# Relation pass of a graph network: eight per-relation comparisons with a lane number written as one comparison with a table

## The chip, the cores and the metric

One NeuronCore of a Trainium2 chip runs the whole program. The metric is the device time of one launch in microseconds; the time of a kernel is the median of its runs.

## What is computed

Four graph layers one after another on 3125 nodes of 64 features and 100000 edges, with a residual and a layer norm behind each: attention (three rounds), an edge MLP with a mean over incoming edges, a relational layer with eight weight matrices, and a graph convolution with signed edge weights. The change touches the third:

```
x_src = x[src]
out = zeros
for r in range(8):
    msg = where(edge_type == r, x_src @ weight[r], 0)
    out = out + segment_sum(msg, dst, num_segments=3125)
out = relu(out + x @ self_loop_w.T)
x = layernorm(x + out)
```

## The kernel before

Edges are sorted once into slots: 13 triples of destination bins by 25 source tiles give 325 chunks of three tiles with 128 slots each (`NCHUNK`, `SLOTS`, `P`). Every later layer runs `edge_pass` over these chunks. For each chunk it must fetch a row per edge, and then add the rows up by destination, which is a matmul with a one-hot matrix of destinations.

In the relation pass (`kind == "relations"`, tag `rp`) a row is x[src] @ weight[type]. Of every five chunks, two are fetched: GpSimd gathers 3 x 128 rows from the table `rel_rows` in DRAM (L1306, 130 chunks, eight slots ahead). The other three (positions 0, 2 and 4 of five, 195 chunks in all) are looked up by TensorE. Their steps are:

- `spell` on TensorE (L1560): three matmuls spread the chunk's 384 keys over all 128 partitions of a PSUM bank. A key is 128 times the relation plus the source node's number within the tile.
- `take_key` on ScalarE (L1487): copies them to `key_rows`, fp16, two buffers.
- `hot_source` on VectorE (L1344): for each relation r compares `key_rows` with the lane number 128 r + p of partition p and writes the one-hot `hot_src`, bf16, eight times 384 columns, two buffers (`HOT_SLOTS`).
- `look_up` on TensorE (L1577): 24 matmuls, 3 tiles by 8 relations, of `hot_src` with `rel_pieces` (each table value in three bf16 parts).
- `take_rows` on ScalarE (L1495, L1497): copies the result to `msg`.
- `hot_target` on VectorE (L1353): the one-hot of destinations, for every chunk. `add_up` on TensorE (L1605, L1607 for looked-up chunks, L1611 for fetched ones) adds up in PSUM.

The order on each engine is written out. In iteration c, TensorE does `spell(c + 6)`, `look_up(c + 3)`, `add_up(c)`; VectorE does `hot_source(c + 3)`, `hot_target(c)`; ScalarE does `take_key(c + 4)`, `take_rows(c + 1)`. Semaphores tie them: `hot_source` of the n-th looked-up chunk waits for `key_taken` of n and for `looked_up` of n - 2; `look_up` waits for `hot_made` of n; `take_key` waits for `spelled` of n and `hot_made` of n - 2; GpSimd waits for `added` of the fetched chunk eight back. Before the loop VectorE waits for the first leftover record, computes `left_number`, and makes the first two one-hots.

Of the kernel before, what the change touches and what calls it, by code (L numbers as in the profile page):

```python
# [5 lines left out]
FP16 = mybir.dt.float16  # L6
# [4 lines left out]
ALU = mybir.AluOpType  # L11
# [3 lines left out]
P = 128  # L15
# [4 lines left out]
RELS = 8  # L20
# [12 lines left out]
SLOTS = 3  # L33
# [129 lines left out]
class Program:  # L163
# [57 lines left out]
    def sb(self, name, shape, dtype=FP32):  # L221
        return self.ctx.enter_context(self.nc.sbuf_tensor(name, shape, dtype))
# [911 lines left out]
def over_columns(a, count):  # L1134

    return a.unsqueeze(2).broadcast_to([a.shape[0], a.shape[1], count])
# [13 lines left out]
def edge_pass(k, tag, kind, pieces, table, width, cols):  # L1150
# [12 lines left out]
    HOT_SLOTS = 2 if relations else 8  # L1163
# [8 lines left out]
    with ExitStack() as ctx, semaphores(nc, tag) as sem:  # L1172
        sb = lambda name, shape, dt=FP32: ctx.enter_context(nc.sbuf_tensor(f"{tag}_{name}", shape, dt))
        described, spelled, hot_made, looked_up = sem("described"), sem("spelled"), sem("hot_made"), sem("looked_up")
# [15 lines left out]
        if relations:  # L1190
            rows = sb("rows", [P, ROW_SLOTS, SLOTS, width])
            key_rows = sb("key_rows", [P, 2, SLOTS * P], FP16)
            hot_src = sb("hot_src", [P, 2, RELS, SLOTS * P], BF16)
            hot_dst16 = sb("hot_dst16", [P, DST_SLOTS, SLOTS, BIN_ROWS], BF16)
            msg = sb("msg", [P, MSG_SLOTS, SLOTS, 3 * D], BF16)
        else:
            hot_src = sb("hot_src", [P, HOT_SLOTS, SLOTS * P], BF16)
            msg = sb("msg", [P, MSG_SLOTS, SLOTS, cols])
# [37 lines left out]
        with nc.Block() as block:  # L1236
# [82 lines left out]
            def _(dve):  # L1319
                v, chain = nc.vector, Chain(dve, step)  # L1320
# [17 lines left out]
                def hot_source(c):  # L1338
                    n = LOOKUP_NO[c]
                    dve.wait_ge(key_taken, n + 1)  # L1340
                    if n >= HOT_SLOTS:
                        dve.wait_ge(looked_up, n - HOT_SLOTS + 1)
                    for rel in range(RELS):
                        last = v.tensor_scalar(hot_src[:, n % HOT_SLOTS, rel, :], key_rows[:, n % 2, :],  # L1344
                                               k.lane[:, rel:rel + 1], None, ALU.is_equal)
                    last.then_inc(hot_made, 1)

                def hot_target(c):
                    if c >= DST_SLOTS:
# [39 lines left out]
                def left_number():  # L1389
                    if relations:  # L1390
                        v.scalar_tensor_tensor(left_no[:, :], left_rec[:, H + 3:H + 4], float(RELS),
                                               left_rec[:, H + 5:H + 6], ALU.mult, ALU.add).then_inc(left_idx, 1)
                    else:
                        v.tensor_copy(left_no[:, :], left_rec[:, H + 3:H + 4]).then_inc(left_idx, 1)
# [39 lines left out]
                dve.wait_ge(left_in, 16)  # L1434
                left_number()
                if relations:
                    for c in range(3):
                        if looks_up(c):
                            hot_source(c)
                if kind == "near":  # L1440
                    weigh(0)
                for c in range(NCHUNK):
                    if edges and c % FILL == 0 and c // FILL + READ_AHEAD < NCHUNK // FILL:
                        describe(c // FILL + READ_AHEAD)
                    if relations and c + 3 < NCHUNK and looks_up(c + 3):
                        hot_source(c + 3)
                    hot_target(c)
                    if kind == "near" and c + 1 < NCHUNK:
                        weigh(c + 1)
                    if not relations:  # L1450
                        message(c)

                left_count = dve.value_load(k.left_tiles[0:1, 0:1], min_val=1, max_val=EPAD // P)
                with dve.Fori(0, left_count) as i:
# [4 lines left out]
                    for b in range(LEFT_BANKS):  # L1459
# [6 lines left out]
                        first, n = 4 * b, min(4, NT - 4 * b)  # L1466
# [3 lines left out]
                        last = v.tensor_tensor(to, to, bank[:, 0:n, 0:main], ALU.add)  # L1470
                    if edges:
                        last = v.tensor_tensor(k.acc[:, :, H:FIELD], k.acc[:, :, H:FIELD],
                                               k.psum[:, 7, 0:NT * 3].rearrange("p (t c) -> p t c", c=3), ALU.add)
# [679 lines left out]
def program(nc, dram, out):  # L2153
    with ExitStack() as ctx:
# [16 lines left out]
        with nc.sbuf_tensor("edge_pieces", [P, NT, 3, FIELD], BF16) as pieces:  # L2171
            edge_table(k, pieces)
            edge_pass(k, "ep", "edges", pieces, k.edge_rows, H, FIELD)
        edge_mean(k)
        node_mlp(k)
        with nc.sbuf_tensor("rel_pieces", [P, looked_up, RELS, 3 * D], BF16) as pieces:
            with nc.sbuf_tensor("rel_rest", [P, LOOKED_UP, RELS * D], FP32) as k.rel_rest:
                relation_table(k, pieces)
            edge_pass(k, "rp", "relations", pieces, k.rel_rows, D, D)
        with nc.sbuf_tensor("near_pieces", [P, NT, 3, D + 2], BF16) as pieces:  # L2180
            with nc.sbuf_tensor("near", [P, NT, D + 2], FP32) as k.near:
                near_table(k, pieces)
            edge_pass(k, "sp", "near", pieces, k.near_rows, D + 2, H)
# [59 lines left out]
```

## Time and profile before

| | us |
|---|---|
| median of 3 runs | 4437.56 (4431.42 to 4444.34) |
| profiled execution | 4402.9 |
| its span | 4401.2 |
| VectorE busy in the span | 3220.0 |
| TensorE matmuls busy in the span | 3083.2 |
| GpSimd busy in the span | 1408.1 |

The relation pass is the stretch from about 2834 to 3495 us of the span. In the rows further down, times are in microseconds from the span's start, PE is TensorE's matmuls, DVE VectorE, ACT ScalarE and POOL GpSimd. A bracket or the part behind a bar tells how long the engine was idle before the instruction and what is thought to have ended that; "issue" means that the view found no releaser. Some semaphore records are missing from a trace, so a real wait can appear as "issue", or under the name of a DMA of another pass.

### The profile page before, as it was taken

The page shows a single profiled execution, that of the slowest core. Times are in us where ns is not written, and L with a number is a line of the kernel's source. Part 1 is how long each engine was busy: PE and PEld are TensorE (multiplying, and loading weights), DVE is VectorE, ACT ScalarE, POOL GpSimd, SP SyncE. Part 2 cuts the span into 40 slices and gives each one's busy share as a digit, 9 for nine tenths or more (in the row PEclk, how much of TensorE's full clock was granted, in tenths as well). Part 3 has the DMA queues.
Part 4 walks back from the last instruction along what each step waited for, and adds up shares of the span by engine and source line. Part 5 has one row for each costly group of instructions (what it writes and reads, how often), then busy time and mean ns, then how long its engine had stood idle before and what let it go on. Part 6 is the DMA issues. An engine that isn't in the chain of part 4 may idle for free. (4 is left out here: it accounts for less than half of the span.)

```text
span 4401.2 us, 85012 instructions
## 1 busy us (share of the span) xinstructions
PE 3083.2 (70%) x29186; PEld 2395.9 (54%) x29186; DVE 3220.0 (73%) x7812; ACT 1438.3 (33%) x2737; POOL 1408.1 (32%) x1203
## 2 busy tenths in 40 slices
PE   0077777787228338338499996588888769968996
PEld 0044554454102102112299995278888759958996
DVE  7766666666389799789577774277777679977887
ACT  0034444444115125125299992233333200000000
POOL 0055555555254464464000000166666300000000
PEclk9988888888569669669699996599999979989998
DMA  8844555545458448458366660111111023313332
GB/s 319 339 129 133 164 149 157 160 132 154 141 168 260 143 136 265 125 162 262 108 216 220 217 207 15 66 23 25 24 24 24 17 66 109 107 41 100 91 90 56
DMA packets 414245, 587.75 MB, mean 134 GB/s; under 512 B 76564, under 2 KB 302443, under 8 KB 413445
## 3 DMA queue, kind: packets, MB, share of 16 engines
q1 hardware_dynamic: 366293, 448.13, 33.9%
q0 software_dynamic: 37888, 67.18, 5.4%
q10 hardware_dynamic: 9648, 67.01, 3.7%
q8 instruction: 247, 4.05, 0.4%
q14 instruction: 169, 1.38, 0.1%
HBM read 340.53 MB, written 235.00 MB: 131 GB/s over the span
## 5 line engine op out<-in xcount | busy, mean ns | idle before, releaser
L848 POOL DMA_INDIRECT slots<-bc_rec,idx x496 | 485.6, 979 | 390.4 <-ACT bc_rec L808 275.3
L1108 PE MATMUL psum<-a_probs,z 128*65 128x512 f32 (+1 forms) x1050 | 448.2, 561 | 141.9 <-DVE a_probs L1041 141.8
L1344 DVE TENSOR_SCALAR rp_hot_src<-rp_key_rows,lane 128x384 bf16<-128x384 f16 x1560 | 382.2, 315 | 175.6 <-issue 80.8
L1577 PE MATMUL psum<-rel_pieces,rp_hot_src 128*128 128x192 bf16 x4680 | 438.7, 248 | 72.6 <-issue 55.6
L1306 POOL DMA_INDIRECT rp_rows<-rel_rows,slot_rel x390 | 410.8, 1053 | 224.0 <-issue 86.5
L1076 ACT ACTIVATE a_tops<-a_tops,a_s_low 128x1024 f32<-128x1024 f32 (+2 forms) x300 | 284.0, 947 | 568.6 <-DVE a_tops L1032 568.3
L484 POOL DMA_INDIRECT slots<-h,idx x192 | 328.9, 1713 | 353.5 <-DMA h<-recs 305.1
L1577 PEld LDWEIGHTS psum<-rel_pieces,rp_hot_src 128*128 128x128 bf16 x4680 | 386.0, 99 | 96.8 <-issue 74.7
L1108 PEld LDWEIGHTS psum<-a_probs,z 128*65 128x65 f32 x1050 | 122.2, 138 | 468.4 <-DVE a_probs L1041 296.6
L704 DVE TENSOR_SCALAR bc_first_t<-bc_ramp,bc_key_t 128x128 f16<-128x128 f16 x500 | 135.3, 271 | 306.0 <-PE psum L730 175.4
L1032 DVE SCALAR_TENSOR_TENSOR a_tops<-table,a_s_rest,big 128x1024 f32<-128x1024 f32 (+2 forms) x300 | 306.9, 1023 | 32.0 <-DMA big<-shift_rows 31.8
L730 PE MATMUL psum<-bc_first_s,bc_first_t 128*128 128x512 f16 x1000 | 217.3, 378 | 111.5 <-DVE bc_first_s L705 62.2
L1041 DVE SCALAR_TENSOR_TENSOR a_probs<-a_tops,a_counts 128x1024 f32<-128x1024 f32 (+2 forms) x300 | 288.2, 962 | 0.0
L1611 PE MATMUL psum<-ep_msg,ep_hot_dst 128*84 128x131 f32 x1950 | 278.3, 278 | 7.7 <-ACT ep_msg L1503 5.8
L1611 PE MATMUL psum<-sp_msg,sp_hot_dst 128*84 128x128 f32 x1950 | 280.0, 280 | 0.0
L1611 PE MATMUL psum<-sq_msg,sq_hot_dst 128*84 128x128 f32 x1950 | 272.4, 276 | 0.0
L1584 PE MATMUL psum<-far_pieces,sq_hot_src 128*128 128x128 bf16 x2925 | 218.1, 220 | 29.5 <-DMA sq_hot_src<-hot_rows 29.5
L705 DVE TENSOR_SCALAR bc_first_s<-bc_ramp,bc_key_s,bc_base_s 128x625 f16<-128x625 f16 x500 | 238.7, 477 | 0.0
L1101 PE MATMUL psum<-ident,a_shifts 128*50 128x128 f32 x3 | 1.2, 410 | 330.5 <-DVE a_shifts L1023 330.5
L1584 PE MATMUL psum<-edge_pieces,ep_hot_src 128*128 128x131 bf16 x2925 | 228.6, 223 | 2.2 <-ACT ep_hot_src L1520 2.2
L1611 PEld LDWEIGHTS psum<-ep_msg,ep_hot_dst 128*84 128x84 f32 x1950 | 221.7, 154 | 10.2 <-DVE ep_hot_dst L1353 9.3
L1374 DVE TENSOR_TENSOR ep_sums<-psum,ep_rec 128x393 f32<-128x393 f32 x325 | 183.7, 565 | 58.6 <-PE psum L1584 58.0
(459 smaller groups left out, 6697.1 us busy)
## 6 DMA issues: line engine op xcount, KB each, us to landing
a_counts<-edge_counts SPq DMA_DIRECT2D x150, 512.0 KB
slots<-big ACTq DMA_DIRECT2D x65, 1005.0 KB
ep_rec<-slots SPq DMA_DIRECT2D x65, 1005.0 KB, 7.5
edge_counts<-bc_counts SPq DMA_DIRECT2D x12, 3125.0 KB
hot_rows<-ep_hot_src SPq DMA_DIRECT2D x325, 96.0 KB, 4.6
sp_hot_src<-hot_rows SPq DMA_DIRECT2D x325, 96.0 KB, 2.1
sq_hot_src<-hot_rows SPq DMA_DIRECT2D x325, 96.0 KB, 2.0
a_counts<-edge_counts SPq DMA_DIRECT2D x75, 282.5 KB
```

Of the source, the lines that this page charges most:

```text
L484: pool.indirect_dma_start(k.slots, bass.IndirectOffsetOnAxis(k.idx[:, at:at + 1], 0), self.rows[y][:, t, :], None).then_inc(self.scattered ...
L705: last = v.tensor_scalar(to_s[:, u, :], ramp[:, :], column(key_s, t), column(base_s, j), ALU.subtract, ALU.is_equal)
L848: pool.indirect_dma_start(k.slots, bass.IndirectOffsetOnAxis(k.idx[:, first + t:first + t + 1], 0), rec[:, j, t, :], None).then_inc(scatte ...
L1032: v.scalar_tensor_tensor(tops[:, cols], shift_1[:, cols], s_rest[:, s:s + 1], shift_2[:, cols], ALU.add, ALU.max).then_inc(topped, 1)
L1041: v.scalar_tensor_tensor(probs[:, cols], tops[:, cols], 1.0, counts[:, cols], ALU.min, ALU.mult)\
L1076: nc.scalar.activation(tops[:, cols], tops[:, cols], ACT.Exp, bias=s_low[:, s:s + 1])\
L1108: last = nc.tensor.matmul(sums[:, a:b], k.z[:, s, 0:D + 1], probs[:, a:b], start=s == 0, stop=True, skip_group_check=True)
L1306: pool.indirect_dma_start(rows[:, n % ROW_SLOTS, s, 0:width], None, table, bass.IndirectOffsetOnAxis(k.slot_rel[:, at:at + 1], 0))\
L1344: last = v.tensor_scalar(hot_src[:, n % HOT_SLOTS, rel, :], key_rows[:, n % 2, :], k.lane[:, rel:rel + 1], None, ALU.is_equal)
L1577: last = nc.tensor.matmul(to, hot_src[:, n % HOT_SLOTS, r, s * P:(s + 1) * P], pieces[:, row, r, :], start=s != 1 and r == 0, stop=True, s ...
L1584: last = nc.tensor.matmul(got[:, s, :], hot_src[:, n % HOT_SLOTS, s * P:(s + 1) * P], pieces[:, row, piece, :], start=s == 0 and piece == ...
L1611: last = nc.tensor.matmul(to[:, 0:D] if relations else to, hot_dst[:, y, s, :], got, start=first, stop=True, skip_group_check=True)
```

## The change

Three edits. A table `lanes` of 8 x 384 fp16 values per partition is added to SBUF. Before the first one-hot, one tensor_copy fills it by repeating each of the eight lane numbers 384 times, and VectorE waits for its end. In `hot_source` the eight tensor_scalars are replaced by one tensor_tensor over 3072 elements per partition: one source is `key_rows`, read eight times over by a broadcast, the other is `lanes`; the result goes to the same `hot_src`. `hot_made` is raised by that one instruction.

```diff
@@ -1191,6 +1191,7 @@
             rows = sb("rows", [P, ROW_SLOTS, SLOTS, width])
             key_rows = sb("key_rows", [P, 2, SLOTS * P], FP16)
             hot_src = sb("hot_src", [P, 2, RELS, SLOTS * P], BF16)
+            lanes = sb("lanes", [P, RELS, SLOTS * P], FP16)
             hot_dst16 = sb("hot_dst16", [P, DST_SLOTS, SLOTS, BIN_ROWS], BF16)
             msg = sb("msg", [P, MSG_SLOTS, SLOTS, 3 * D], BF16)
         else:
@@ -1340,10 +1341,9 @@
                     dve.wait_ge(key_taken, n + 1)
                     if n >= HOT_SLOTS:
                         dve.wait_ge(looked_up, n - HOT_SLOTS + 1)
-                    for rel in range(RELS):
-                        last = v.tensor_scalar(hot_src[:, n % HOT_SLOTS, rel, :], key_rows[:, n % 2, :],
-                                               k.lane[:, rel:rel + 1], None, ALU.is_equal)
-                    last.then_inc(hot_made, 1)
+                    shape = [P, RELS, SLOTS * P]
+                    v.tensor_tensor(hot_src[:, n % HOT_SLOTS, :, :], key_rows[:, n % 2, :].unsqueeze(1).broadcast_to(shape),
+                                    lanes[:, :, :], ALU.is_equal).then_inc(hot_made, 1)
 
                 def hot_target(c):
                     if c >= DST_SLOTS:
@@ -1434,6 +1434,7 @@
                 dve.wait_ge(left_in, 16)
                 left_number()
                 if relations:
+                    chain.link(v.tensor_copy(lanes[:, :, :], over_columns(k.lane[:, :], SLOTS * P)))
                     for c in range(3):
                         if looks_up(c):
                             hot_source(c)
```

`over_columns(a, count)` repeats each column of a `count` times by a broadcast (step 0 innermost).

## Rows read from the trace of the kernel before

**Rows 1.** The page, busy tenths of PE and DVE in 40 slices.
```profile
PE   0077777787228338338499996588888769968996
...
DVE  7766666666389799789577774277777679977887
```

**Rows 2.** Busy time by stretch: window, its length, engines with instruction counts, clock, DMA.
```profile
2854.00:2869.00 15.00, 2.59 (x10) 1.63 (x11) 2.58 (x10) 0.75 (x3) 9.04 (x10) 0.50 0.12 23
2900.00:3465.00 565.00, 496.28 (x6377) 470.86 (x6376) 426.85 (x1661) 201.55 (x527) 364.56 (x345) 1.00 0.11 25
3471.00:3490.00 19.00, 19.00 (x261) 19.00 (x261) 17.42 (x70) 8.14 (x23) 0.00 (x0) 1.00 0.01 3
```

**Rows 3.** Groups by line and form, 2834 to 3495: busy us, mean ns, idle before.
```profile
L1577 PE MATMUL psum<-rel_pieces,rp_hot_src 128*128 128x192 bf16 x4680 | 438.7, 248 | 72.6 <-issue 55.6 <-DVE rp_hot_src L1344 15.7
L1306 POOL DMA_INDIRECT rp_rows<-rel_rows,slot_rel x390 | 410.8, 1053 | 224.0 <-issue 86.5 <-PE psum L1611 85.4 <-DMA rel_rows<-big 52.2
...
L1344 DVE TENSOR_SCALAR rp_hot_src<-rp_key_rows,lane 128x384 bf16<-128x384 f16 x1560 | 382.2, 315 | 175.6 <-issue 80.8 <-DMA marks_now<-edge_marks 57.3 <-ACT rp_key_rows L1487 35.7
```

**Rows 4.** Timeline of DVE, one period: start, length, instruction, count, idle before.
```profile
3158.97 1.95 DVE L1344 TENSOR_SCALAR rp_hot_src<-rp_key_rows,lane 128x384 bf16<-128x384 f16 x8 [2.38 <-issue]
3160.84 0.41 DVE L1353 TENSOR_TENSOR rp_hot_dst<-bin_lane,slot_dst 128x252 f32<-128x252 f32 x1
3161.17 1.91 DVE L1344 TENSOR_SCALAR rp_hot_src<-rp_key_rows,lane 128x384 bf16<-128x384 f16 x8
...
3168.70 1.95 DVE L1344 TENSOR_SCALAR rp_hot_src<-rp_key_rows,lane 128x384 bf16<-128x384 f16 x8 [2.46 <-issue]
```

**Rows 5.** Timeline of PE in the same period.
```profile
3160.97 2.15 PE L1577 MATMUL psum<-rel_pieces,rp_hot_src 128*128 128x192 bf16 x24 [1.21 <-issue]
...
3166.29 0.33 PE L1560 MATMUL psum<-ident,slot_key 128*128 128x128 f16 x3
...
3170.70 0.51 PE L1577 MATMUL psum<-rel_pieces,rp_hot_src 128*128 128x192 bf16 x4 [1.34 <-issue]
```

**Rows 6.** Timeline of PE: first and last of the 47 lookups behind their comparisons.
```profile
2876.91 0.83 PE L1577 MATMUL psum<-rel_pieces,rp_hot_src 128*128 128x192 bf16 x8 [0.21 <-issue]
...
3468.55 0.67 PE L1577 MATMUL psum<-rel_pieces,rp_hot_src 128*128 128x192 bf16 x6 [1.20 <-issue]
```

**Rows 7.** Timeline of ACT in the period, the key copies.
```profile
3158.44 0.87 ACT L1487 ACTIVATE rp_key_rows<-psum 128x384 f16<-128x384 f32 x2 [1.50 <-PE psum L1560]
...
3168.17 0.87 ACT L1487 ACTIVATE rp_key_rows<-psum 128x384 f16<-128x384 f32 x2 [0.74 <-DMA marks_now<-edge_marks]
```

**Rows 8.** Single lines of DVE: count, shortest/median/longest in ns, first and last start.
```profile
L1344 DVE TENSOR_SCALAR rp_hot_src<-rp_key_rows,lane x1560: 299/309/526, 2834.0 to 3492.3; 128x384 bf16<-128x384 f16 x195
...
L1353 DVE TENSOR_TENSOR rp_hot_dst<-bin_lane,slot_dst x325: 400/407/417, 2837.7 to 3493.5; 128x252 bf16<-128x252 f32 x99, 128x252 f32<-128x252 f32 x64
...
L1407 DVE TENSOR_SCALAR big<-all_rows,rp_left_rec x1: 1047/1047/1047, 3493.9 to 3493.9; 128x3200 bf16<-128x3200 int16 x1
...
L1940 DVE TENSOR_TENSOR edge_pieces<-big,edge_pieces x1: 3493/3493/3493, 2169.6 to 2169.6; 128x3200 bf16<-128x3200 f32 x1
```

**Rows 9.** Timeline of PE, two lookups a period apart after the last gather.
```profile
3471.06 2.14 PE L1577 MATMUL psum<-rel_pieces,rp_hot_src 128*128 128x192 bf16 x24
...
3479.22 2.14 PE L1577 MATMUL psum<-rel_pieces,rp_hot_src 128*128 128x192 bf16 x24
```

**Rows 10.** Two casts of DVE from 32 to 16 bits.
```profile
L2047 DVE CAST rel_pieces<-rel_rest x5: 959/959/960, 2758.8 to 2828.2; 128x1536 bf16<-128x1536 f32 x5
...
L1937 DVE CAST edge_pieces<-table x1: 3465/3465/3465, 2159.0 to 2159.0; 128x3200 bf16<-128x3200 f32 x1
```

**Rows 11.** Timeline of DVE, the first comparisons of the pass.
```profile
2834.04 3.78 DVE L1344 TENSOR_SCALAR rp_hot_src<-rp_key_rows,lane 128x384 bf16<-128x384 f16 x16
```

**Rows 12.** Timeline of POOL in the period, two gathers.
```profile
3161.35 1.85 POOL L1306 DMA_INDIRECT rp_rows<-rel_rows,slot_rel  x1 [0.30 <-issue]
3163.85 0.94 POOL L1306 DMA_INDIRECT rp_rows<-rel_rows,slot_rel  x1 [0.65 <-PE psum L1611]
```

## The prediction

> **What bounds the kernel now.** I read the page's slices first. The edit touches one pass only, the relation pass, which fills about 660 us of the 4401 us span; in its slices TensorE (PE) and VectorE (DVE) are both high and neither is full [rows 1]. The chain that ended last covers the final layer alone, so it can't price this pass. Next the busy time by stretch: between 2900 and 3465 us PE is busy 496.28 of 565 us and DVE 426.85 us, at a granted clock of 1.00 [rows 2]. So PE stands idle 68.7 us there, and no faster DVE can give back more than what of that idleness is a wait for DVE. The groups by form give the sizes: the 1560 comparisons of L1344 fill 382.2 us, that is 1.96 us for each of the 195 groups of eight; PE is idle 72.6 us before its lookup matmuls; the gathers of GpSimd (POOL) take 1053 ns on average [rows 3].
>
> Then the timeline of one period (five chunks, three looked up). DVE compares in groups of eight: 3158.97 for 1.95 us, the next at 3161.17, and the pattern comes again at 3168.70 [rows 4]. A period is thus 9.73 us. PE starts a lookup at 3160.97, 0.05 us after the first of those groups ends (3158.97 + 1.95 = 3160.92), after 1.21 us of idleness; at 3170.70 the same after 1.34 us (3168.70 + 1.95 = 3170.65) [rows 5]. The view names "issue" there; by the times it is the hot_made wait of `look_up`. The two other groups of a period end well before their lookups. I counted this through the pass: 47 of the 195 lookups, at most one in a period of 65, start within 0.1 us of the end of their comparisons after an idle stretch, 46.0 us in all; the first and the last are shown [rows 6]. Two more at the start of a period add 3.1 us.
>
> Why is that group late? It starts right behind the key copy of ScalarE (ACT): copies at 3158.44 and 3168.17, comparisons 0.53 us later. And the copy itself waited: 1.50 us for L1560 before 3158.44 [rows 7], although PE had issued the last spelling of a period at, for instance, 3166.29 for 0.33 us [rows 5] and the copy came at 3168.17 [rows 7]. PE's signals come late here. They do so only while POOL gathers: after the last gather, from 3471 to 3490, PE is busy 19.00 of 19 us with POOL at 0.00 [rows 2], and a period is 3479.22 - 3471.06 = 8.16 us [rows 9].
> So the loop is: lookup, spelling, late signal, key copy, comparisons, lookup. The comparisons count once in it, in 47 of 65 periods.
>
> **The change part by part.** *Eight tensor_scalars out.* One takes 309 ns at the median for 384 elements, and L1407 takes 1047 ns for 3200 [rows 8]: (1047 - 309) / 2816 = 0.26 ns an element, so each pays some 0.10 us for data and 0.13 us of its 0.23 us spacing for being an instruction (1.87 us from 3158.97 to 3160.84, by eight) [rows 4]. What goes is 1.96 us a group, with the disturbed ones in it.
>
> *One tensor_tensor of 3072 elements in.* The trace holds no tensor_tensor whose operands are all of 16 bits. With a 32-bit operand, 252 elements take 407 ns and 3200 take 3493 ns [rows 8]: 1.047 ns an element and 0.144 us fixed. At that rate 3072 elements take 3.36 us. At two elements in that time they take 1.61 + 0.14 = 1.75 us. These are the two ends: 1.75 and 3.36 us. Nothing in the trace suggests a form below 1.75 (that would be the rate of tensor_scalar). I take 1.75: the tensor_scalars with 16-bit operands run four elements in the time in which the mixed forms run one, so packing of 16-bit values is at work in this program, both sources have step 1 innermost, and the width change alone should give the factor of two. That choice is the weak point and is the first rival.
>
> The Trainium skill bears on it twice. Its page VectorE: DVE Perf Modes, section on the perf-mode tier table, speaks against the edit: tensor_scalar of 16 bits may reach 4x, tensor_tensor only 2x. The trace agrees on the first half (0.26 against 1.047 ns an element), and by the rule the data part doubles from 0.8 to 1.6 us while seven fixed costs go. The Vector Engine (DVE) Microarchitecture Reference, section 5.1, adds that a row read again and again as a source of a two-source instruction kept the 2x mode; no row here shows that.
>
> The gain on DVE: 1.96 - 1.75 = 0.21 us a group, 41 us over 195. On the path lie 47 + 2 groups: 49 x 0.21 = 10.3 us. The other 146 groups are covered by PE's own work; making them shorter is free time on DVE, which is idle over a fifth of the pass anyway. If that cover is gone, they are worth at most 0.21 us each, 31 us more; nothing in the trace removes it. Once the late group is 0.21 us shorter, it is still last: the idle time before the 47 lookups is 0.98 us on average, so the wait shrinks and doesn't vanish.
>
> *Waits.* The wait on key_taken and on looked_up stay in front, and hot_made is raised once at the end as before. `take_key` waits for hot_made of an earlier group; that comes 0.21 us sooner too, and its own bound is the spelling.
>
> *The table of lanes.* One tensor_copy of 3072 elements from 32 to 16 bits in front of the first comparisons, with a wait for its end. Nearest rows: a cast of 1536 elements 959 ns, one of 3200 elements 3465 ns [rows 10], so 1.8 us at the faster rate (twice 0.96, less a fixed part) and 3.36 us at the slower. I take 3.36: it reads one element over and over. The first group now starts at 2834.04 [rows 11] with its key ready, so the delay is on the path: nothing else of the pass but POOL's gathers runs by then. Only `left_number` stays ahead of it, so POOL isn't delayed. Right behind come 15 us in which PE does 2.59 us of work while POOL fills its slots [rows 2]; that stretch could swallow the delay, so the bounds are 0 and 3.4 us. SBUF is taken (6 KB a partition), which costs no time.
>
> *Sum.* 3.4 - 10.3 = -6.9 us. The profiled execution takes 4402.9 us (4401.2 of span), and becomes 4396. It lies 34.7 us under the median of the runs, 4437.56. I carry the difference over: 4430.7 us, 0.16% down. A measurement of this kernel can tell about 0.3%, 13 us, from no change.
>
> **The rivals.** *Slower: one element at a time* (chance 0.08). The broadcast source or the mixed fp16-to-bf16 types keep the tensor_tensor at the rate of the mixed forms: 3.36 us, about 3.28 in spacing. DVE then needs 3 x 3.28 + 5 x 0.33 = 11.5 us a period and becomes the bound; with some of the key wait left up to 12.3. Against 9.73 that is 1.8 to 2.6 us in 65 periods, 117 to 169 us; middle 143, so 4580 us. The edit loses from 2.0 us upward: beyond 1.96 us the 49 groups cost more than now, and the break-even with the table is 1.96 - 3.4 / 49 = 1.89 us.
>
> *No gain: the wait refills* (0.20). The late signals from PE are tied to the gathers, not to the comparisons. If the signal that frees the key copy then comes as late as before on the clock, the period stays 9.73 us and only the table is left: 4441 us. For it: the lateness is 1.5 us and more, many times the 0.21 us in question. Against it: the gathers start on PE's own `added`, so the whole loop should move with it.
>
> *Relief for the gathers* (0.15). A gather starting at 3161.35, inside a group of comparisons, took 1.85 us, the next 0.94 [rows 12]; comparisons reach 526 ns against 309 [rows 8]. The two disturb each other. The tensor_tensors of L1353 never exceed 417 ns [rows 8]. If the new form leaves POOL alone, the mean gather goes from 1053 to about 940 ns, 0.68 us a period over six gathers, and if PE's late signals shorten by the same: some 40 us, 4400 us. Were they to vanish, the period would be 8.16 us and the time 4345 us. Against it: between 2854 and 2869 PE crawls with DVE busy 2.58 of 15 us [rows 2], so the comparisons aren't what delays PE.
>
> *Collision with the gathers* (0.06). A tensor_tensor held for 1.75 us could block a gather, or wait for one (0.94 us), on about half the groups: 49 x 0.5 x 0.94 = 23 us, 4455 us with the table. Against it stands the 417 ns of L1353. The Trainium skill's page SBUF — State Buffer, section "Who interferes with whom", says that a DVE instruction with two SBUF inputs contends with GpSimd instructions that read SBUF; by it this rival would be the likelier one, and the trace's short tensor_tensors speak against it.
>
> **How the numbers follow.** Forecast 0.51, the rivals 0.08, 0.20, 0.15 and 0.06. The forecast's own spread is 4420 to 4438 (table at 0 or 3.4 us, some of the covered groups on the path, 3 us of scatter of a median), of which 0.13 lies beyond -0.3%. Faster by over 0.3%: 0.13 + 0.15 = 0.28. Slower: 0.08 + 0.06 = 0.14. Within: 0.58. The range leaves out the one-at-a-time case, the far end of the relief and half of the collision: 4395 to 4450.
>
> **What would show it.** The new row's mean: 1.75 us right, 3.36 the first rival. The period: 9.5 us right, 9.73 the second, 9.1 or less the third. Idle time before L1577: down from 72.6 by some 10 us. The mean gather: 1053 ns if nothing changed there. The table's copy: 3.4 us before the first comparisons. The prediction is wrong if a tensor_tensor of 16 bits isn't packed, or if PE's late signals depend on what DVE does.

## The result: slower, and the profile after

The changed kernel takes 4481.01 us (median; 4475.53 to 4484.68) where the kernel before, in the same session, takes 4440.95 us (4431.42 to 4447.77): a ratio of 1.0084, 95% interval 1.0069 to 1.0099. The forecast was 4430.7 us with a range up to 4450. The sign was wrong. The profiled execution has a span of 4481.9 us; its relation pass, from the issue of the load of the first leftover record to the end of the last lookup, takes 715.4 us, against 662.8 us before.

The page of the changed kernel, to be held against [rows 1]: in the slices of the pass POOL now stands at 7 and 8 tenths where it had 6, and the granted clock, which was full there, falls to 0.8 and 0.9. POOL and clock on the page before were:

```profile
POOL 0055555555254464464000000166666300000000
PEclk9988888888569669669699996599999979989998
```

And after:

```profile
PE   0087777877238348248499995677987859978996
...
DVE  7766666665489789689577773455665659977887
...
POOL 0055555555264454554000000477877700000000
PEclk9988888888569679579699995688988969988998
```

The groups by form, which answer to [rows 3] (lines are one higher than before). The new instruction takes 1758 ns, as forecast. The gathers go from a mean of 1053 to 1468 ns and POOL's idle time before them from 224.0 to 140.5 us. PE is idle 53.4 us before it adds fetched rows up, 38.5 of them for their arrival; before the change it was 22.5 us, and none of it was put down to the rows.

```profile
L1307 POOL DMA_INDIRECT rp_rows<-rel_rows,slot_rel x390 | 572.5, 1468 | 140.5 <-issue 111.2 <-PE psum L1612 16.5 <-DMA rel_rows<-big 7.8
L1578 PE MATMUL psum<-rel_pieces,rp_hot_src 128*128 128x192 bf16 x4680 | 454.3, 254 | 48.3 <-issue 42.9 <-DVE rp_hot_src L1345 4.6
...
L1345 DVE TENSOR_TENSOR rp_hot_src<-rp_key_rows,rp_lanes 128x3072 bf16<-128x3072 f16 x195 | 342.7, 1758 | 257.0 <-ACT rp_key_rows L1488 92.0 <-PE psum L1578 82.2 <-DMA marks_now<-edge_marks 50.0
...
L1612 PE MATMUL psum<-rp_rows,rp_hot_dst 128*84 128x64 f32 x780 | 84.1, 242 | 53.4 <-DMA rp_rows<-rel_rows,slot_rel 38.5 <-issue 8.3 <-DVE rp_hot_dst L1353 6.0
```

DVE's and POOL's timelines of about one period, to be held against [rows 4] and [rows 12]:

```profile
3156.01 1.76 DVE L1345 TENSOR_TENSOR rp_hot_src<-rp_key_rows,rp_lanes 128x3072 bf16<-128x3072 f16 x1 [1.04 <-ACT rp_key_rows L1488]
...
3158.02 1.75 DVE L1345 TENSOR_TENSOR rp_hot_src<-rp_key_rows,rp_lanes 128x3072 bf16<-128x3072 f16 x1
...
3160.71 1.76 DVE L1345 TENSOR_TENSOR rp_hot_src<-rp_key_rows,rp_lanes 128x3072 bf16<-128x3072 f16 x1 [0.28 <-PE psum L1578]
...
3164.18 1.76 DVE L1345 TENSOR_TENSOR rp_hot_src<-rp_key_rows,rp_lanes 128x3072 bf16<-128x3072 f16 x1 [1.05 <-ACT rp_key_rows L1488]
```

```profile
3156.67 1.92 POOL L1307 DMA_INDIRECT rp_rows<-rel_rows,slot_rel  x1 [0.30 <-issue]
3158.89 1.69 POOL L1307 DMA_INDIRECT rp_rows<-rel_rows,slot_rel  x1 [0.30 <-issue]
3160.89 2.39 POOL L1307 DMA_INDIRECT rp_rows<-rel_rows,slot_rel  x1 [0.30 <-issue]
3163.59 0.94 POOL L1307 DMA_INDIRECT rp_rows<-rel_rows,slot_rel  x1 [0.30 <-issue]
3164.84 1.91 POOL L1307 DMA_INDIRECT rp_rows<-rel_rows,slot_rel  x1 [0.30 <-issue]
```

Take the ends. The tensor_tensors end at 3157.77, 3159.77, 3162.47 and 3165.94; the gathers that started inside them end at 3158.59, 3160.58, 3163.28 and 3166.75: each time 0.81 to 0.82 us later. The gather that started between two of them takes 0.94 us. So a gather that starts inside the long instruction behaves as if it stood still until that instruction ends and then did its remaining 0.8 us. Counted over the pass, 195 gathers start inside a tensor_tensor and average 1.99 us, and 192 of them end 0.81 to 0.83 us after it; the other 195 average 0.95. And from 3156.67 to 3164.84, one period of 8.17 us, POOL does four gathers, where a period needs six. POOL leaves only its 0.30 us between them, here and in 382 of the 389 gaps of the pass: it has become the bound. The 390 gathers with such a gap each make 691 us, the seven longer gaps add 22 us, and the pass begins 5 us ahead of the first gather: together 717 us (rounded parts), of which 2 lie behind the last lookup, and so the 715 us of the pass.

The busy time by stretch shows the other half, to be held against [rows 2]. In the same 565 us DVE is busy 80 us less than before and PE 37 us less; part of that is that less work gets done in them (5599 matmuls where there were 6377). The second line is a stretch of 36 us, one of four in the pass, in which POOL catches up (25 gathers) and PE does only 93 matmuls; the kernel before has one such stretch, at its start [rows 2].

```profile
2900.00:3465.00 565.00, 459.00 (x5599) 430.99 (x5598) 346.29 (x404) 178.24 (x464) 448.61 (x312) 0.89 0.10 22
2935.00:2971.00 36.00, 15.41 (x93) 9.46 (x93) 4.54 (x6) 2.92 (x8) 25.36 (x25) 0.63 0.12 24
```

Between those stretches most periods (37 of the 64 in the pass) take 8.2 us, a pace that PE had before in 4 of the 64, two of them with POOL silent [rows 9]. POOL starts four gathers in each of these periods but one, so its lead of eight slots (24 gathers) melts by two a period, then comes the slow stretch of 36 to 39 us. Of the 80.7 us between the two profiled spans the pass accounts for 52.6; 24.0 us lie ahead of it, where the kernels are the same (the profiled execution before was 34.7 us under its median). The medians differ by 40.1 us, less than the two passes do; with one trace of each it isn't known how much of the 52.6 is scatter.

### The profile page after: what moved, and what is told of

It reads as the page before. It is cut to its first block and busy times, and to the rows that moved or that the text cites. A ratio compares the mean times of both kernels' runs of the same rounds, so it can differ in the third digit from the quotient of the medians.

```text
span 4481.9 us, 83649 instructions
## 1 busy us (share of the span) xinstructions
PE 3114.6 (69%) x29186; PEld 2425.3 (54%) x29186; DVE 3184.9 (71%) x6448; ACT 1437.7 (32%) x2737; POOL 1569.6 (35%) x1203
## 5 line engine op out<-in xcount | busy, mean ns | idle before, releaser
L1307 POOL DMA_INDIRECT rp_rows<-rel_rows,slot_rel x390 | 572.5, 1468 | 140.5 <-issue 111.2
L1345 DVE TENSOR_TENSOR rp_hot_src<-rp_key_rows,rp_lanes 128x3072 bf16<-128x3072 f16 x195 | 342.7, 1758 | 257.0 <-ACT rp_key_rows L1488 92.0
L1578 PE MATMUL psum<-rel_pieces,rp_hot_src 128*128 128x192 bf16 x4680 | 454.3, 254 | 48.3 <-issue 42.9
L484 POOL DMA_INDIRECT slots<-h,idx x192 | 327.3, 1705 | 351.8 <-DMA h<-recs 303.3
L1578 PEld LDWEIGHTS psum<-rel_pieces,rp_hot_src 128*128 128x128 bf16 x4680 | 401.6, 101 | 68.5 <-issue 60.9
L793 ACT ACTIVATE bc_counts<-psum 128x625 f32<-128x625 f32 x125 | 88.1, 705 | 448.3 <-PE psum L740 207.1
```

The lines of the kernel that those rows point to most:

```text
L484: pool.indirect_dma_start(k.slots, bass.IndirectOffsetOnAxis(k.idx[:, at:at + 1], 0), self.rows[y][:, t, :], None).then_inc(self.scattered ...
L1307: pool.indirect_dma_start(rows[:, n % ROW_SLOTS, s, 0:width], None, table, bass.IndirectOffsetOnAxis(k.slot_rel[:, at:at + 1], 0))\
L1345: v.tensor_tensor(hot_src[:, n % HOT_SLOTS, :, :], key_rows[:, n % 2, :].unsqueeze(1).broadcast_to(shape), lanes[:, :, :], ALU.is_equal).t ...
L1578: last = nc.tensor.matmul(to, hot_src[:, n % HOT_SLOTS, r, s * P:(s + 1) * P], pieces[:, row, r, :], start=s != 1 and r == 0, stop=True, s ...
```

## The experiments

Kernels that ran together shared a chip, and the times differ between the chips. The first four ran beside a kernel before at 4436.54 us, the level of the result; the later ones on three other chips where the kernel before took 4121.3, 4123.07 and 4124.92 us. Differences are taken within a session only. "Pass" is the relation pass as above. Theory at the outset: the tensor_tensor's second source takes something that gathers need, so POOL becomes the bound. Rivals: any long instruction of DVE does it; or POOL isn't the bound and the slow stretches are the loss.

**Without gathers, before and after.** All 390 gathers out, the rows they fetch replaced by zeros, and PE's wait for rows lowered to that one signal, so the fetched edges are left out of the result:

```diff
-                        pool.indirect_dma_start(rows[:, n % ROW_SLOTS, s, 0:width], None, table,
-                                                bass.IndirectOffsetOnAxis(k.slot_rel[:, at:at + 1], 0))\
-                            .then_inc(rows_in[n % ROW_SLOTS], 16)
...
+                for y in range(ROW_SLOTS):
+                    nc.gpsimd.memset(rows[:, y, :, :], 0.0).then_inc(rows_in[y], 1)
```

> The kernel before without the 390 gathers of the relation pass (the fetched rows are zeros, so the fetched edges are missing from the layer). Both theories: with no gather running PE's signals come on time, no lookup waits for its comparisons except the first, and every period is as after the last gather of before, 8.16 us; the pass takes about 65 x 8.16 = 531 us instead of 661, the kernel about 130 us less than before. If the late signals of PE had another cause than the gathers, the period stays at 9.7 us.

> The changed kernel without the 390 gathers (the same edges missing). Theory 1 (the tensor_tensor holds a read port that the gathers need, gathers went from 1053 to 1468 ns, POOL became the bound of the pass): without gathers the tensor_tensor costs nothing, the pass takes 531 to 535 us, the same as the kernel before without gathers to within 3 us. Rival (the tensor_tensor itself slows the loop of PE, DVE and ACT in some way): it stays at least 20 us above the kernel before without gathers.

Measured: 4293.18 and 4285.04 us, passes of 537.3 and 536.9 us, every period but the first 8.2 us. PE is busy all the time in the changed kernel too:

```profile
2900.00:3365.00 465.00, 465.00 (x6325) 465.00 (x6324) 389.71 (x457) 200.82 (x525) 0.00 (x0) 1.00 0.02 5
```

So by itself the new instruction costs nothing, and 537 us is PE's floor. What the change costs needs the gathers, and so did PE's late signals of the forecast.

**A memset in its place.** Half the one-hot is set to zero by one instruction without sources (the rest once, ahead of the pass); all looked-up rows are left out by that.

```diff
-                    v.tensor_tensor(hot_src[:, n % HOT_SLOTS, :, :], key_rows[:, n % 2, :].unsqueeze(1).broadcast_to(shape),
-                                    lanes[:, :, :], ALU.is_equal).then_inc(hot_made, 1)
+                    v.memset(hot_src[:, n % HOT_SLOTS, 0:4, :], 0.0).then_inc(hot_made, 1)
```

> The changed kernel with the tensor_tensor replaced by a memset of 1536 elements (about 1.7 us, a DVE instruction of the same length without any source; the one-hots are zeros, so the looked-up edges are missing). Theory 1 (the sources of the tensor_tensor hold a port): the gathers fall back from 1468 ns to 940 to 1000 ns on average. Rival (any long DVE instruction, or the denser schedule, holds the gathers up): they stay at 1300 to 1500 ns. If fast gathers are what makes PE's signals late, periods lie at 9.5 us and more here, although DVE does nothing but memsets.

```profile
L1307 POOL DMA_INDIRECT rp_rows<-rel_rows,slot_rel x390 | 441.2, 1131 | 200.0 <-issue 93.6 <-PE psum L1611 71.1 <-DMA rel_rows<-big 34.7
...
L1344 DVE MEMSET rp_hot_src<- 128x768 uint32 x195 | 136.1, 698 | 416.8 <-ACT rp_key_rows L1487 125.8 <-DMA marks_now<-edge_marks 116.2 <-issue 97.5
```

4424.52 us, pass 669.8. The control was shorter than meant, 698 ns, so it can't part length from sources. Nor did it leave the gathers alone: 96 start inside a memset and average 1.52 us. A tensor_tensor of `hot_target` follows directly on the memset, and 94 of the 96 end 0.81 to 0.82 us after that one, as here, where it ends at 3015.45 and the gather at 3016.27:

```profile
3014.48 0.70 DVE L1344 MEMSET rp_hot_src<- 128x768 uint32 x1 [1.62 <-ACT rp_key_rows L1487]
3015.09 0.36 DVE L1351 TENSOR_TENSOR rp_hot_dst<-bin_lane,slot_dst 128x252 f32<-128x252 f32 x1
```

```profile
3014.90 1.37 POOL L1307 DMA_INDIRECT rp_rows<-rel_rows,slot_rel  x1 [0.30 <-issue]
```

Which of the two held them isn't shown. The run does show that PE's signals stay late with DVE busy 224 of 641 us (427 of 565 before, [rows 2]): the eight comparisons aren't what makes them late.

**Four quarters.** The same comparison cut in four tensor_tensors of 768 elements (the halves and the 6 + 2 cut below are written the same way):

```diff
+                    for r in range(0, RELS, 2):
+                        last = v.tensor_tensor(hot_src[:, n % HOT_SLOTS, r:r + 2, :],
+                                               key_rows[:, n % 2, :].unsqueeze(1).broadcast_to(shape),
+                                               lanes[:, r:r + 2, :], ALU.is_equal)
+                    last.then_inc(hot_made, 1)
```

> The changed kernel with the one tensor_tensor of 3072 elements as four of 768. By the sizes measured each takes 0.40 + 0.14 us, in 0.47 us of spacing, so a group takes 1.94 us, as the eight tensor_scalars did. Theory 1 with the port given back between instructions: a gather waits for one short instruction at most, the mean falls from 1468 to under 1150 ns, POOL needs under 570 us for its gathers, and the kernel is 40 us or more faster than the changed one. Theory 1 with the port kept through instructions that follow directly: the mean stays at 1400 ns and the time within 15 us of the changed kernel.

```profile
L1307 POOL DMA_INDIRECT rp_rows<-rel_rows,slot_rel x390 | 430.6, 1104 | 236.0 <-PE psum L1615 107.3 <-issue 90.6 <-DMA rel_rows<-big 38.1
...
L1346 DVE TENSOR_TENSOR rp_hot_src<-rp_key_rows,rp_lanes 128x768 bf16<-128x768 f16 x780 | 383.9, 554 | 203.6 <-DMA marks_now<-edge_marks 109.8 <-issue 57.9 <-ACT rp_key_rows L1491 29.9
```

4455.68 us, ratio 1.0043 (1.0029 to 1.0058), pass 696.1. The gathers are relieved (1104 ns) although the sources are the same: the hold goes with the single instruction, except for 11 of the 390 gathers, which take 2.6 to 3.4 us, longer than a whole group of quarters. By the two ratios this is some 18 us below the changed kernel, where I expected 40 or more. PE idles 89.1 us before its lookups (48.3 in the changed kernel), as if its late signals were back; that these are what keeps the time up was not tested.

**A copy of the same length.** The lane numbers are copied over the one-hot, one source, about the same length; the one-hots are left out, so the looked-up rows are too.

```diff
-                    v.tensor_tensor(hot_src[:, n % HOT_SLOTS, :, :], key_rows[:, n % 2, :].unsqueeze(1).broadcast_to(shape),
-                                    lanes[:, :, :], ALU.is_equal).then_inc(hot_made, 1)
+                    v.tensor_copy(hot_src[:, n % HOT_SLOTS, :, :],
+                                  over_columns(k.lane[:, :], SLOTS * P)).then_inc(hot_made, 1)
```

> The changed kernel with its tensor_tensor replaced by a copy of the eight lane numbers, each repeated 384 times, into the same 3072 bf16 elements: one VectorE instruction of about 1.75 us (the same copy into the table took 1.75 us), with one source from SBUF instead of two. The looked-up rows are wrong, as the one-hots are left out. If the second source is what holds the gathers back (my theory), the gathers come back to 1053 to 1130 ns on average, the pass to 660-670 us and the time to about 4425-4440 us. If any VectorE instruction of that length holds a gather (rival: length, not sources), the gathers stay near 1450 ns, the pass near 715 us and the time near 4480 us.

```profile
L1307 POOL DMA_INDIRECT rp_rows<-rel_rows,slot_rel x390 | 621.6, 1594 | 118.8 <-issue 109.7 <-PE psum L1607 9.1
...
L1344 DVE CAST rp_hot_src<-lane 128x3072 bf16<-128x3072 f32 x195 | 352.6, 1809 | 277.5 <-PE psum L1577 176.7 <-ACT rp_key_rows L1487 99.6
```

4338.34 us beside 4121.3, pass 745.5. My theory that it takes a second source falls: with one source the gathers are longer still. The copy also holds gathers that had begun before it: those in which a copy starts average 1.62 us over 129, where those in which a tensor_tensor starts average 0.94 in the changed kernel (77 of them). All 40 that begin less than 0.5 us before their copy end 0.12 us after it. The Trainium skill's page SBUF — State Buffer, section "Who interferes with whom", says that a cast in a two-port mode takes the pair of ports shared with GpSimd for the whole instruction, and that a tensor_tensor takes only the pair's read interface, which the page calls inferred; these figures fit that and don't prove it.

**Gathers spread out.** Each of a chunk's three gathers waits for one more added chunk, in the kernel before and in the changed one.

```diff
-                    if n >= ROW_SLOTS:
-                        pool.wait_ge(added, FETCHES[n - ROW_SLOTS] + 1)
                     for s in range(SLOTS):
+                        if n >= ROW_SLOTS:
+                            pool.wait_ge(added, FETCHES[n - ROW_SLOTS] + 1 + s)
+                        elif n >= 2:
+                            pool.wait_ge(added, c - 5 + s)
```

> The kernel before with its gathers spread out: each of a chunk's three gathers now waits for one more added chunk (instead of all three for one), and the first ones too are tied to the adds. Theory (PE's late signals and the slow stretch at the start come with gathers issued back to back at 1.25 us): the 33 us stretch at the start shrinks to some 10 us and part of the late signals goes, time 4400 to 4425 us. Rival (any gather delays PE, whatever its spacing, since 390 of them must still run): no change, 4435 to 4445 us. If the spread gathers come too late for their adds, PE waits for rows and the time is above 4450 us.

> The changed kernel with the same spreading of the gathers. Theory: the four slow stretches of 36 to 39 us against 8.2 us for a usual period go, which is 4 x 29 = 116 us, but POOL stays the bound with 390 gathers of 1.47 + 0.30 to 0.36 us = 690 to 713 us, so that PE waits for rows instead; the pass stays at 690 to 715 us and the time at 4455 to 4480 us. Rival (POOL isn't the bound, the slow stretches cost the time by themselves): the pass falls to 600 to 640 us and the time to 4370 to 4400 us.

Before, spread: 4126.36 us, ratio 1.0006 (0.9991 to 1.0022). After, spread: 4292.63 us, ratio 1.0406 (1.0376 to 1.0436), pass 710.5, gathers 1512 ns. Neither tested what it was made for, because on this chip there are no late signals: the first says nothing on them, and the slow stretches are missing from the changed kernel there without any spreading too ("The changed kernel on another chip", below). What it does show is a pass as long as ever without one slow stretch (no period above 13 us). So the loss doesn't need the stretches; on the chip of the result POOL's own sum, above, says that they are where it was paid.

**The table alone**, added to the kernel before, read by nobody.

> The kernel before with nothing but the table of lane numbers added: its copy of 3072 elements in front of the first comparisons, and nobody reads it. The forecast had 3.4 us for it, with bounds 0 and 3.4; the copy itself took 1.75 us in the changed kernel. Theory: 0 to 1.8 us more than before, not distinguishable. Rival (the 15 to 30 us more of the profiled execution ahead of and at the start of the pass come from the table, through its place in SBUF or the later start): 15 us or more above before.

4122.14 us, ratio 1.0001 (0.9985 to 1.0017): free. It also gives the profile of the old comparisons on this kind of chip: pass 539.4 us, PE full, and POOL too. None of POOL's 389 gaps is above 0.35 us, and its gathers fill 536.0 us from first to last: here the kernel before has no slack on POOL at all.

```profile
2700.00:3180.00 480.00, 478.34 (x6496) 477.73 (x6495) 439.77 (x1700) 205.52 (x537) 373.63 (x349) 1.00 0.14 29
```

```profile
L1307 POOL DMA_INDIRECT rp_rows<-rel_rows,slot_rel x390 | 417.5, 1070 | 118.9 <-issue 115.5 <-PE psum L1613 2.1 <-PE psum L1609 1.2
```

**The changed kernel on another chip.**

> The changed kernel once more, on another chip of the same kind, beside the kernel before. On the first chip the pass took 662.8 us before and 715.4 us after. On the second the kernel before (with the unused table) passed in 539.4 us, close to the 537 us without gathers, so TensorE's late signals are missing there, while the gathers behind a long VectorE instruction stayed long (1512 and 1594 ns). Theory (POOL's gathers are the bound of the changed kernel, 390 at 1.83 us): the pass takes about 710 us on either chip; where the kernel before takes 540, the change costs 170 us, a ratio of 1.04, and where it takes 663, 1.008. Rival (the loss belongs to the first chip alone): ratio at or below 1.01 wherever the kernel before is at 4120 us.

```profile
L1307 POOL DMA_INDIRECT rp_rows<-rel_rows,slot_rel x390 | 579.7, 1486 | 118.8 <-issue 107.6 <-PE psum L1608 11.3
...
L1612 PE MATMUL psum<-rp_rows,rp_hot_dst 128*84 128x64 f32 x780 | 80.8, 240 | 117.5 <-DMA rp_rows<-rel_rows,slot_rel 108.5 <-DVE rp_hot_dst L1353 8.5
```

4290.98 beside 4123.07 us: ratio 1.0398 (1.0369 to 1.0426), pass 703.0. The pass of the changed kernel is POOL's on either kind of chip (715 and 703 us), and mainly the kernel before differs (663 and 539). Here it shows plainly: PE waits 108.5 us for rows.

**One element at a time, same length.** 1536 elements with a 32-bit table, two sources; the one-hots of relations 4 to 7 stay zero, which leaves those edges out.

```diff
-                    v.tensor_tensor(hot_src[:, n % HOT_SLOTS, :, :], key_rows[:, n % 2, :].unsqueeze(1).broadcast_to(shape),
-                                    lanes[:, :, :], ALU.is_equal).then_inc(hot_made, 1)
+                    v.tensor_tensor(hot_src[:, n % HOT_SLOTS, 0:4, :], key_rows[:, n % 2, :].unsqueeze(1).broadcast_to(shape),
+                                    over_columns(k.lane[:, 0:4], SLOTS * P), ALU.is_equal).then_inc(hot_made, 1)
```

> The changed kernel with its tensor_tensor of 3072 elements, all of 16 bits, replaced by one over 1536 elements whose table is read as 32-bit lane numbers (relations 0 to 3 only; the one-hots of relations 4 to 7 are left at zero, so those edges' rows are left out): by 1.047 ns an element and 0.144 us fixed it takes the same 1.75 us, with two sources from SBUF, one element at a time. If it is the length that holds the gathers back, their mean is again 1450 to 1600 ns and the pass 710 to 745 us. If it is the packed mode (two elements at a time; the copy of lane numbers was packed too and gave 1594 ns), the gathers come back to 940 to 1000 ns and the pass is where the kernel before has it or below (540 or 660 us by chip).

```profile
L1307 POOL DMA_INDIRECT rp_rows<-rel_rows,slot_rel x390 | 586.9, 1505 | 118.9 <-issue 107.3 <-PE psum L1609 11.6
...
L1345 DVE TENSOR_TENSOR rp_hot_src<-rp_key_rows,lane 128x1536 bf16<-128x1536 f16 x195 | 342.8, 1758 | 250.3 <-PE psum L1579 176.7 <-ACT rp_key_rows L1489 73.6
```

4292.72 beside 4123.07 us, pass 707.8. Same length, half the elements, no packing: same loss. For a tensor_tensor the length of one instruction counts, not the packing.

**Two halves**, and then the halves timed:

> The changed kernel with the tensor_tensor cut in two of 1536 elements, some 0.9 us each. Where the gather waits for the end of the instruction it meets, the delay falls with the square of the length for the same work: mean gathers were 1053 ns beside eight of 0.31 us, 1104 beside four of 0.55 us, 1468 beside one of 1.76 us; by that two give 1150 to 1250 ns and a pass of 560 to 600 us where TensorE isn't late, 680 to 700 us where it is. Rival (a gather is held by the whole group of comparisons, however cut): 1400 ns or more.

> The changed kernel with the tensor_tensor in two halves, timed against the kernel before. On a chip without late TensorE signals: 541 us of pass, a ratio of 0.998 to 1.002, since TensorE bounds the pass at 8.16 us a period whatever VectorE does. On a chip with late signals (before near 4437 us): by the theory that each held gather costs POOL time and that PE's lateness is the gathers' doing, between the quarters' 1.0043 and 1.00; the rival, that lateness grows with the length of VectorE's instructions, gives 1.006 or more.

The rows are those of the timed run:

```profile
L1307 POOL DMA_INDIRECT rp_rows<-rel_rows,slot_rel x390 | 418.1, 1072 | 118.8 <-issue 110.3 <-PE psum L1615 8.5
...
L1346 DVE TENSOR_TENSOR rp_hot_src<-rp_key_rows,rp_lanes 128x1536 bf16<-128x1536 f16 x390 | 358.3, 960 | 70.1 <-ACT rp_key_rows L1491 62.4 <-PE psum L1581 4.8
```

4122.9 us, and timed 4123.97 us: ratio 0.9996 (0.9986 to 1.0007), pass 541 us in both. Cutting the instruction once gives back the whole 4%. The gathers are below the 1150 to 1250 ns that I expected, and the pass below the 560 to 600 us. Of the 198 gathers that start inside a half, over 50 start in its first 0.01 us and aren't held.

**Six and two relations**, as a test of the hold:

> The changed kernel with the tensor_tensor cut into one of six relations (2304 elements, by 0.52 ns an element and 0.16 us fixed some 1.36 us) and one of two (0.56 us). In the trace of the changed kernel a gather that starts inside the tensor_tensor ends 0.8 us after it, 0.94 us after its own start otherwise. Theory (hold until the end of the one instruction met, the rest of the instruction at most): 195 gathers are held by at most 1.2 us instead of 1.6, about half as often at their start; mean gather 1150 to 1300 ns. With 0.30 us between gathers POOL needs 390 x 1.45 to 1.6 = 565 to 625 us, against 541 us of pass with halves: 4150 to 4210 us where the kernel before takes 4123. Rival (a threshold: gathers are held only beyond some length above 1.36 us): mean near 1075 ns, pass 541 us, no loss.

Two gathers of this kernel and the instructions they started in; at 3003.04 the view merges the two parts, 1.36 and 0.55 us:

```profile
3003.59 1.62 POOL L1307 DMA_INDIRECT rp_rows<-rel_rows,slot_rel  x1 [0.30 <-PE psum L1610]
...
3009.48 1.91 POOL L1307 DMA_INDIRECT rp_rows<-rel_rows,slot_rel  x1 [0.30 <-issue]
```

```profile
3003.04 1.83 DVE L1345 TENSOR_TENSOR rp_hot_src<-rp_key_rows,rp_lanes 128x2304 bf16<-128x2304 f16 x2 [1.01 <-PE psum L1580]
...
3009.22 1.36 DVE L1345 TENSOR_TENSOR rp_hot_src<-rp_key_rows,rp_lanes 128x2304 bf16<-128x2304 f16 x1 [0.98 <-ACT rp_key_rows L1490]
```

```profile
L1307 POOL DMA_INDIRECT rp_rows<-rel_rows,slot_rel x390 | 484.0, 1241 | 118.9 <-issue 103.6 <-PE psum L1610 15.2
```

3003.04 + 1.36 = 3004.40, and the gather ends at 3005.21; 3009.22 + 1.36 = 3010.58, and it ends at 3011.39: 0.81 us later both times. 4190.74 beside 4124.92 us, pass 604.8, within what the hold predicted (4150 to 4210); the threshold falls. The gather of 3003.59 ends by the first part although the second follows directly: the hold is the single instruction's.

**The sum that holds.** An unheld gather is 0.945 us and POOL needs 0.305 us between two (118.9 us of idle time over 390), so 390 take 487 us. Add what the gathers that start inside a comparison lose (their count times their mean above 0.945, counted in each trace):

| kernel (other chips) | start inside, loss | POOL needs, us | pass, us |
|---|---|---|---|
| halves | 198 x 0.25 | 537 | 541 |
| 6 + 2 | 195 x 0.59 | 602 | 605 |
| changed | 202 x 1.04 | 698 | 703 |
| one at a time | 196 x 1.11 | 705 | 708 |

The sum is built from the same traces as the pass, so it is an account and no forecast; what it shows is that POOL has no other idle time, since the pass also begins some 5 us ahead of the first gather. PE's floor is 537 us, so the halves are just free, and everything longer is POOL's. The old comparisons cost POOL 536 us in the same way.

**Spread once more**, in the hope of a chip with late signals, which it didn't meet:

> The kernel before with its gathers spread out, once more. On a chip without late signals nothing changes (pass 540 to 545 us). On a chip with late signals: if gathers back to back make TensorE late, the 33 us stretch at the start of the pass goes and the pass is 600 to 640 us instead of 663; if each gather does it whatever its neighbours, 655 to 665 us.

4140.12 us beside 4124.92, pass 548.0, in a single run and just above the 540 to 545 us expected; nothing on the lateness.

## Why the prediction was wrong

*The instruction itself* was right: 1.75 us forecast, 1758 ns measured, two elements in the time of one. The rival "one element at a time" is out.

*The table* was mis-sized: 3.4 us forecast, 1.75 measured (first line below), in the time not to be seen. The wide broadcast ran at the faster rate of [rows 10].

```profile
2857.99 1.75 DVE L1437 CAST rp_lanes<-lane 128x3072 f16<-128x3072 f32 x1
2859.77 3.43 DVE L1345 TENSOR_TENSOR rp_hot_src<-rp_key_rows,rp_lanes 128x3072 bf16<-128x3072 f16 x2
```

*The gain, 49 x 0.21 = 10.3 us*, has no place to show. The reading of the loop was right as far as it went (many periods do fall to 8.2 us), but the period is no longer set by it.

*The step that failed* is "Collision with the gathers". The forecast gave it a chance of 0.06 and 23 us. Three things in it were wrong. The evidence: that L1353 never exceeds 417 ns [rows 8] says that DVE isn't held by gathers, and I read it as if it said that gathers aren't held by DVE; and L1353 is short besides. The row that bore on it was [rows 12], 1.85 us inside a group of comparisons against 0.94 outside: DVE does hold gathers. (That one ends 0.12 us after the eighth short instruction, 3163.20 against 3163.08; 30 of the 390 before take 1.68 us or more, so short instructions back to back can hold a gather together, if seldom.) The place: I priced it at DVE's 49 late groups, 23 us, instead of at POOL, for all 195 groups. The bound: "what bounds the kernel now" never worked out POOL's own need. From [rows 3] and the 0.30 us of [rows 12] it was 390 x (1.053 + 0.30) = 528 us of 662.8, a slack of 135 us. One gather held for a mean of 1.04 us by each of 195 instructions is 203 us on top of 487, 690 us: past the slack. On the chip of the result the pass went from 662.8 to 715.4 us; where PE's signals aren't late there was no slack to begin with, and it went from 539 to 703. The Trainium skill's section named in the prediction had the collision right, though no size for it, and the prediction let a row about the wrong side outweigh it.

*"Relief for the gathers"* had the sign reversed: 1053 ns became 1468, not 940. Two of the rivals' prices are also off by their own figures: 65 periods of 8.16 instead of 9.73 us are 102 us less and give about 4339 us, not 4345, and 23 us on the forecast give 4454, not 4455; neither changes the verdict. *"No gain"* was right that the late signals hang on the gathers and not on the comparisons, as the runs without gathers and with the memset show; that they would hold the period at 9.73 us is not what happened.

*What stays open.* Why PE's signals come late beside gathers in the sessions of the result and the first four runs and not on the other chips. No chip was met in two of the experiments' sessions, so chip and session aren't told apart. The same difference stands in another stage with gathers, ahead of the pass and untouched by the change: POOL waits 390.4 us there on the one chip and 219.7 us on the other (kernel before, then the one with the unused table).

```profile
L848 POOL DMA_INDIRECT slots<-bc_rec,idx x496 | 485.6, 979 | 390.4 <-ACT bc_rec L808 275.3 <-issue 115.1
```

```profile
L848 POOL DMA_INDIRECT slots<-bc_rec,idx x496 | 485.0, 978 | 219.7 <-issue 118.6 <-ACT bc_rec L808 101.2
```

A third stage with gathers, L484 with 288 of them, takes the same on both, 976.9 and 977.5 us from the first to the last. Behind the pass the two take 906.2 and 911.5 us (from the last lookup to the end of the span). Nor is it shown what makes quarters cost 0.4% on the first chip; the halves never ran on a chip of that kind, so that they are free there isn't shown.

No version that computes the whole result beat the kernel before: on the other chips before and halves both stand at PE's floor.

## What to carry to other kernels

Merging short VectorE instructions into a long one made each of them a wall for GpSimd's gathers here: price it as one gather held for the rest of the instruction, times their count, against GpSimd's own slack, gap between gathers included. An engine whose profile shows it idle can have no slack left once the duration of one of its instructions plus the gap behind it is multiplied by their count: with the old comparisons GpSimd was busy 373.63 of 480 us on the other chips and had none. If the merge is wanted, stop at a length whose holds fit the slack; here two halves of 0.96 us did and 1.36 us did not.

## What the runs showed of the hardware

- A gather that starts inside a tensor_tensor of 0.96, 1.36 or 1.76 us ends 0.81 to 0.83 us after it, packed or not (192 of 195 in the changed kernel, 195 of 195 beside 1.36 us); started before it, or in its first 0.01 us, it takes its usual 0.94 us. Short instructions back to back sometimes hold one longer (30 of 390 before, 11 of 390 beside quarters). A copy of 1.8 us also holds those that began up to 0.5 us before it (all 40, to 0.12 us after its end).
- A tensor_tensor of 3072 elements, all 16 bits, one source read eight times over, takes 1758 ns; 2304 take 1358, 1536 take 960, 768 take 554.
- The same program takes 4437 us on one chip and 4121 to 4125 on three others, and in the two traces at hand the difference lies in two of the three stages in which GpSimd gathers. The same change costs 0.84% on the one and 3.98% on another.
- In a slow stretch (36 us with 93 matmuls) TensorE's granted clock averages 0.63, between its two levels of 1.2 and 2.4 GHz; from 2900 to 3465 us it is 0.89, against 1.00 before [rows 2], and a lookup's matmul takes 254 ns instead of 248. Since POOL bounds that pass, no run shows that the lower clock costs time there.
